# AdaLN transformer block with routed experts: the closing operations of batch 6 move from VectorE to GpSimd, and one addition of batch 4 moves ahead of the last tile

## What is computed

```
mod = (silu(c) @ wmod).reshape(8, 6, 1, -1)     # sa, ca, ga, sb, cb, gb
h = layernorm(x) * (1 + ca) + sa
x = x + ga * attention(h)
h = layernorm(x) * (1 + cb) + sb
x = x + gb * (routed(h) + shared(h))            # 2 of 8 experts for each token
```

## Time and profile before

| | before |
|---|---|
| median of 3 runs (lowest to highest) | 278.69 us (278.34 to 280.42) |
| time of the profiled execution | 280.89 us |
| its span in the trace | 278.9 us |
| granted TensorE clock, mean | 0.993 |
| busy: PE, DVE, ACT, POOL | 254.6, 202.8, 161.4, 132.1 us |

### The profile page before, as it was taken

The page is one execution under the profiler, slowest core; times in us unless marked ns, Lnnn a source line. Parts: engine busy times, 40 slices in busy tenths (PEclk is TensorE's granted clock), DMA queues, the critical chain, the costliest instruction groups (busy, mean ns, idle before and its releaser), DMA issues.

```text
span 278.9 us, 6194 instructions
## 1 busy us (share of the span) xinstructions
PE 254.6 (91%) x1797; PEld 235.3 (84%) x1797; DVE 202.8 (73%) x632; ACT 161.4 (58%) x429; POOL 132.1 (47%) x148
## 2 busy tenths in 40 slices
PE   0889999898999999999999889989999999999980
PEld 0787778797989999998979778989999999999960
DVE  1675974147998674388479778466899978989986
ACT  2447558968655754836536375355666666666630
POOL 4120313744255037785895375600455645555650
PEclk9999999999999999999999999999999999999997
DMA  7795007154224102242134023525754367485663
GB/s 230 272 346 160 0 7 228 49 158 125 74 66 127 47 1 98 95 124 86 67 119 139 34 84 123 202 81 130 199 151 129 123 205 235 135 239 211 227 190 118
DMA packets 28175, 37.89 MB, mean 136 GB/s; under 512 B 4476, under 2 KB 20711, under 8 KB 28144
## 3 DMA queue, kind: packets, MB, share of 16 engines
q1 hardware_dynamic: 23648, 28.63, 34.2%
q0 software_dynamic: 3216, 8.46, 8.1%
q10 hardware_dynamic: 1280, 0.41, 0.6%
HBM read 25.18 MB, written 12.71 MB: 136 GB/s over the span
## 4 chain that ended last, share of the span: by engine, by line
PE 70%; DVE 12%; issue 6%; ACT 4%; POOL 2%; DMA 2%; ACTq 1%; DVEq 0%; SPq 0%; POOLq 0%
PE bank L348 15%; PE bank L350 14%; PE bank L349 14%; PE bank L1148 4%; PE bank L1120 3%; PE bank L1367 3%; PE bank L1140 2%; PE bank L1103 2%; PE bank L1131 2%; PE bank L1112 2%; PE bank L1021 1%; PE bank L1398 1%; PE bank L1397 1%; DVE h2T_lo L1442 1%; DMA h2all<-routed_in 1%
## 5 line engine op out<-in xcount | busy, mean ns | idle before, releaser
L1496 POOL DMA_INDIRECT routed_out<-yo_all,dest x35 | 38.6, 1102 | 44.2 <-ACT yo_all L1438 32.1
L711 POOL DMA_INDIRECT routed_in<-h2all,slot_u x32 | 31.6, 986 | 21.8 <-DVE slot_u L692 11.6
L348 PE MATMUL bank<-experts_w,h2T_lo 128*128 x117 | 39.7, 339 | 0.1
L350 PE MATMUL bank<-experts_w,h2T_hi 128*128 x117 | 36.2, 309 | 0.0
L349 PE MATMUL bank<-experts_w,h2T_hi 128*128 x117 | 36.0, 307 | 0.0
L348 PE MATMUL bank<-h2T_hi,wsgu_lo 128*128 128x256 f32 (+1 forms) x96 | 27.9, 290 | 0.7 <-ACT og L482 0.7
L350 PE MATMUL bank<-h2T_hi,wsgu_hi 128*128 128x256 f32 (+1 forms) x96 | 27.0, 281 | 0.0
L349 PE MATMUL bank<-h2T_lo,wsgu_hi 128*128 128x256 f32 (+1 forms) x96 | 26.9, 281 | 0.0
L1422 ACT ACTIVATE wstage<-bank 128x176 f32<-128x176 f32 x39 | 12.4, 318 | 22.1 <-PE bank L350 22.1
L348 PEld LDWEIGHTS bank<-experts_w,h2T_lo 128*128 128x128 f32 x117 | 22.2, 190 | 0.8 <-issue 0.6
L349 PEld LDWEIGHTS bank<-experts_w,h2T_hi 128*128 128x128 f32 x117 | 22.3, 190 | 0.0
(11 more groups left out here) (278 smaller groups left out, 827.8 us busy)
## 6 DMA issues: line engine op xcount, KB each, us to landing
h2all<-routed_in SPq DMA_DIRECT2D x39, 130.0 KB, 2.5
wstage<-gu_t SPq DMA_DIRECT2D x8, 352.0 KB, 3.2
res<-x SPq DMA_DIRECT2D x4, 512.0 KB, 8.9
mx_all<-modrow SPq DMA_DIRECT2D x8, 256.0 KB, 3.2
mh_all<-modrow SPq DMA_DIRECT2D x8, 256.0 KB, 3.4
exchange<-routed_out SPq DMA_DIRECT2D x4, 512.0 KB, 4.8
wmod_s<-w_mod SPq DMA_DIRECT2D x3, 512.0 KB, 10.0
out<-res SPq DMA_DIRECT2D x6, 256.0 KB, 3.1
```

What stands on the lines that cost most here:

```text
L348: pe.matmul(out_ap, l[1], r[0], start=start, stop=False)
L350: return pe.matmul(out_ap, l[0], r[0], start=False, stop=stop)
L711: pool.indirect_dma_start(out=routed_in, out_offset=bass.IndirectOffsetOnAxis(slot_u[:, i, j:j + 1], 0), in_=h2all[:, j % (2 * NB), :], in ...
L1496: pool.indirect_dma_start(out=routed_out, out_offset=bass.IndirectOffsetOnAxis(dest[:, t % 16:t % 16 + 1], 0), in_=yo[t % 6], in_offset=No ...
```

## The change

GpSimd closes batch 6 as well as batch 5, and `FIN_AT` has one more step, 37. The list `ROWS` is thereby 15 long instead of 18, and all 15 have a step: the 15th, "out" of batch 4, stands at the end of the step of tile 37. No operation, shape, transfer or buffer is changed.

```diff
-            BY_POOL = (5,)
+            BY_POOL = (5, 6)
-                    FIN_AT = (20, 21, 22, 23, 24, 25, 28, 29, 30, 31, 32, 33, 35, 36)
+                    FIN_AT = (20, 21, 22, 23, 24, 25, 28, 29, 30, 31, 32, 33, 35, 36, 37)
```

## The result

The change made the kernel slower: the median of 15 runs is 282.08 us against 280.29 for 15 runs of the kernel before, a ratio of 1.0083 with a 95% interval of 1.0056 to 1.0111. (The kernel before was run again beside it; its first three runs, shown ahead, had a median of 278.69.

A forecast was written before the change was run, and what follows sets the result against it. The prediction took VectorE's tail and the last store as the bound: 2.79 us off, 0.30 on, then load 7 and mutual waiting left 0.83 gained. From the median of 278.69 it forecast 277.9 us, range 276.7 to 279.2.

The forecast's parts named there:

- What bounds the kernel: Last 7.0 us, after TensorE's last matmul: VectorE's operations to 276.72, then the last store; GpSimd idle from 269.40.
- VectorE's end decides: End of the kernel: VectorE ends at 275.89 instead of 276.72, so the span falls by 0.83 us.
- The rivals: No mutual waiting, 276.9 (0.15); load 7 pays for store 4, 278.5 (0.08); GpSimd first at 268, 277.9 (0.12); slower (0.12).
- the slower one: Tail: GpSimd keeps batch 7's "sum" out until batch 6 is done; 0.3 us slower, far bound 1.6; chance 0.12.
- What leaves the path: VectorE's tail: four operations of batches 4 and 6 ahead of batch 7's "sum" go, at most 2.79 us.
- the moved addition: "Out" of batch 4, now at 268.00 on VectorE: shifts everything up to VectorE's last tile sum by 0.30 us.
- The two engines wait for each other: Tail: VectorE and GpSimd operations with two SBUF inputs don't run side by side; gain near 0.8 us, without this 1.8.
- the prediction's own sign: Batch 7's "sum" on VectorE: about 1.5 us expected; if 0.69, the waiting is wrong and 276.9 is right.
- The loads: Load 6 lands at 270.04, load 7 at 271.83, with store 4 costing load 7 nothing; 2.00 us is left.
- The numbers: Chances against the kernel before: within 1% 0.95, faster by over that 0.03, slower by over that 0.02.

The follow-up runs named there:

- the kernel with one drain: The changed kernel with one GpSimd drain added between the scatters of the first and last stage: ratio 0.9967 to the kernel before.
- both runs with a late memset: The kernel before with a very late 128 x 8 GpSimd memset: ratio 1.0144; the same with a drain ahead of the memset: 1.0027.
- the control with one drain: The kernel before with one GpSimd drain added between the scatters of the first and last stage: ratio 0.9988.
- middle way: Against the kernel before: step 37 added, only "sum" of batch 6 on GpSimd, batch 7's "sum" between VectorE's other two; ratio 0.9962, then 0.9986.
- both of its parts alone: The kernel before with only step 37 added: ratio 0.9988; with only batch 6 moved to GpSimd: ratio 1.0091.
- the part without step 37: The kernel before with only batch 6 moved to GpSimd, "out" of batch 4 staying behind the last tile: ratio 1.0091.
- the kernel with drains alone: A kernel without the whole computation, GpSimd draining behind memsets, an addition, and 1, 4 and 12 landed scatters: drains 0.15, 0.40, 1.03 us behind the scatter groups' memsets.

## Why the prediction was wrong

**What bounds the kernel.** The tail was read rightly as VectorE's, for the kernel before. What was missing is the second chain beside it. The earlier trace rows were read as "GpSimd is done at 269.40 and idle for 9.5 us". It was idle in its busy rows; its queue was in the drain until 275.0, and from there to SP's end at 278.7 only 3.7 us were free. This is the step that failed, and with it the sum "VectorE's end decides": the end is the later of the last store's landing and GpSimd's last operation plus 5.57 us. With the forecast's own time for that operation, 274.47, the drain would have ended at 280.04 and the span at about 280.3: slower than 278.9 by 1.4 us, where 0.8 were forecast as gained. The rivals had no such case either; the slower one put the loss in GpSimd keeping VectorE's "sum" out until batch 6 was done, which didn't happen.

**What leaves the path, and the moved addition.** 2.79 us off and 0.30 on. After, TensorE's chain for tile 38 shifted as forecast: the low halves started 0.94 behind the moved addition (forecast 268.94 - 268.00). The last tile sum came 2.99 behind it, 0.29 more than the 2.70 of the earlier trace rows. Right.

**The two engines wait for each other.** Right as a mechanism, wrong in the order. "Out" of batch 5 took 1.72 us beside the moved addition (forecast near 1.7), and VectorE was first there, by 0.11. At 272.85 VectorE's "sum" of batch 7 was first by 0.1 and GpSimd's "scale" took 1.72; at 274.87 VectorE's second half of "scale" met GpSimd's "out" (274.81 to 276.07) and ended at 276.35, in the timeline from 275 on:

```profile
274.87 1.48 DVE L1593 TENSOR_TENSOR mh_all<-mh_all,sact 128x256 f32<-128x256 f32 x1
```

The forecast had GpSimd's "scale" first and batch 7's "sum" and GpSimd's "out" held up, to about 1.5 us each; they took 0.69 and 1.26. By the prediction's own sign a "sum" of 0.69 meant that there is no waiting; the sign was too narrow, since the waiting came later, in the two halves of batch 7's "scale". VectorE's waits hardly changed in sum: from the landing of load 7 to its end it took 4.06 us in the forecast and about 4.2 in the trace, where 2.89 is what it takes without waiting. That "late", which reads one input from PSUM, isn't held up was stated from the earlier trace rows, which don't show it; the trace after does, with 0.75 us for its two halves from 273.64 on, beside GpSimd's "scale". As the Trainium skill says of the shared pair of ports ("SBUF — State Buffer", section "SBUF: two separate sides"), the one that starts first has it for the whole instruction; these rows agree, with 0.4 us more for GpSimd and 1.1 for VectorE.

**The loads.** Mis-sized. The profiled execution after was 0.43 us late from before the tail on (last scatter at 264.21 instead of 263.78). On top, SP issued load 6 at 267.62, 3.41 behind the start of the last scatter, where the earlier trace rows had 2.36; it landed about 1.0 later than that shift accounts for, and load 7 about 0.6 later. With the shift VectorE ended 1.13 later than forecast (277.02 against 275.89) and GpSimd 1.60 later (276.07 against 274.47), so that this execution would show no gain even without the drain. What SP waits for ahead of load 6 is the landing of the last scatter. In the kernel before that came 2.2 us behind the scatter's start, in the kernel with one drain 3.8 behind; the trace of the changed kernel lacks that landing, but SP waited 6.2 us there instead of 5.1. Why the scatter lands later isn't known. In the kernels without drains in the last stage, SP issued load 6 2.35 or 2.36 us behind the last scatter's start in the kernel before, in both runs with a late memset, in the control with one drain and in the first middle way, and 3.4 to 4.1 behind it in the changed kernel, in both of its parts alone, in the changed one with one drain and in the second run of the middle way. One and the same kernel, the middle way, thus stands in both groups, and each run has one trace: the lateness can't be put down to the change. In the first group the issue of load 7 behind it took 1.28 to 1.58 us instead of 0.36, so load 7 left SP at most 0.8 us earlier. It isn't store 4, as the part without step 37 has it too.

**The numbers.** Within 1% was given 0.95, and the ratio is within 1%; but the sign and the range were wrong: the bounds were all drawn from busy rows, and the closing drain stands in none.

## What to carry to other kernels

Before giving late work to an engine that seems idle at the end, read what its queue does after its last operation, not only its busy rows: the time by which it may end later is counted to the end of its closing drain. On GpSimd the drain grew here with the indirect transfers issued since the last drain, 0.081 us for each, and one drain in an idle stretch took their part off the end; behind a scatter that was still under way, or ahead of the next one, a drain was dear. Of two changes that are each forecast to gain a few tenths of a microsecond, one lost over 2 us beside the path that the forecast had followed, and trying one part at a time showed which.

## What the hardware showed that was not expected

- GpSimd's closing drain ended 5.56 to 5.57 us behind the last operation in kernels with 67 indirect transfers, 2.94 with 35 since the last drain, 0.31 with 3, 0.05 to 0.08 with none; in the kernel with drains alone, 0.15, 0.40 and 1.03 us for 1, 4 and 12. It doesn't shrink by waiting: 7 us of idle time ahead of it changed nothing.
- A drain directly behind a scatter lasted until 0.07 us behind that scatter's landing, 2.45 us at least in all, and the next scatter started 0.8 us or more behind the drain.
- A VectorE operation of 0.42 us that met GpSimd's addition ended 0.28 us behind the end of that one, at 276.35; it was kept out for all the rest of it.
